# Cross-attention and a two-of-eight expert layer on one core: the hand-over between the two reordered, the places of the rows worked out on two engines

## The chip, the cores and the metric

One Trainium2 chip, one of its cores. The metric is the device time of one launch in microseconds (us): lower is better. The engines are TensorE (PE; its weight loads are listed as PEld), VectorE (DVE), ScalarE (ACT), GpSimd (POOL) and SyncE (SP, which here only issues DMAs). Each engine runs its own instructions in order and waits on semaphores for the others.

## What is computed

```python
# x: 16 x 112 x 256 rows, ctx: 16 x 375 x 256, mask: 16 x 375
x = x + attention(layernorm(x), ctx, ctx, mask, Wq, bq, Wk, bk, Wv, bv, Wo, bo)   # 16 heads of 16
flat = layernorm(x).reshape(1792, 256)
probs = softmax(flat @ router_w)                       # 8 experts
topk_w, topk_idx = top_k(probs, 2)
topk_w = topk_w / clip(topk_w.sum(-1), 1e-9)
h = silu(einsum('td,edf->etf', flat, w1))              # w1: 8 x 256 x 512
y = einsum('etf,efd->etd', h, w2)                      # w2: 8 x 512 x 256
x = x + sum over the two chosen experts of y * topk_w
```

All of it is fp32; products are made from a high and a low part of each operand (three products for one).

## The kernel before

The kernel has three stages. In the first (to about 280 us of the profile) 16 batches pass through an attention pipeline; `turn(b)` on each engine is one batch's share of a software pipeline, in which PE makes the maximum pass of batch b+1 (`head_scores`), the scores and outputs of batch b (`quad_scores`, `quad_outputs`, four of each) and the output projection of earlier rows (`project_output`). In the last stage (from about 366 us) 21 expert steps of 256 gathered rows each run on PE, ACT and DVE, with gathers and scatters issued by POOL.

The stage between them is what the change is about. The 1792 rows lie as 14 tiles of 128 rows. They are taken in eight units: six of two tiles, two of one (`UNITS`, line 63). A unit goes through these steps, each in order on its engine:

- PE `project_output(u)` (L1393 is the line of `product`, which issues nearly all matmuls), DVE `residual(u)` (L1091) adds it to `x2`.
- DVE `row_stats` (L1098) and `row_vars` (L1106, L1108) make mean and variance. They are made in four `GROUPS` (line 64): units 0 to 3 together, then 4 and 5, then 6, then 7. POOL `roots(g)` (L652) takes the roots of a group.
- POOL `normalise_rows(u)` (L661) writes units 0 to 5 into one of three buffers `xn2`, DVE `normalise_late(u)` (L1140) units 6 and 7. SP `write_rows` (L510) writes them to DRAM, where the expert steps gather them.
- PE `flat_transpose(u)` (L1546), ACT `flat_high(u)` (L860), DVE `flat_low(u)` (L1146), PE `route(u)` (six matmuls of 8 columns a tile), DVE `read_logits(u)` (L1152).

Then come the choices and the places. DVE `find_two` (L1173 to L1182, the helper `first_of` at L1166 to L1169) finds the two experts of each row, for the early tiles (the first `EARLY_NT` = 12) and for the late ones (2). PE `rank_early` and `rank_late` (L1677, L1680, L1690 to L1694) count rows before each row of the same expert. DVE `place_rows` (L1200 to L1209) turns that into a lane (a block of 128 places) and a place in it. Both are turned into matrices of zeros and ones: `placed`, one instruction for each tile and choice, 28 in all, by POOL `lanes` (L670), and `is_place` by DVE `places_in_block` (L1214). PE `fill_lanes` multiplies them (L1705, 28 matmuls into one bank). Then DVE `read_lanes` (L1238), PE `list_rows` (L1713) and DVE `list_tokens` (L1243, L1244) give the list by which POOL `gather_rows` (L706) fetches rows.

What sets the order is written by hand: each engine's list of calls behind its attention turns (DVE from L1312, PE and ACT likewise). On PE the list of the last turn alternates attention and router calls; on PE its tail is:

```python
            route(6)
            rank_early()
            flat_transpose(7)
            route(7)
            fill_lanes(slice(0, EARLY_NT))
            rank_late()
            fill_lanes(slice(EARLY_NT, NT))
            list_rows()
```

So `rank_late` stands behind the early `fill_lanes` on PE, and that waits for all of POOL's early lanes: POOL signals `lanes_ready` once for each part. SP loads all experts' weights in two DMAs of 4 MB, the first when the last scores are made, the second behind the writes of units 4 and 5.

## Time and profile before

| | us |
|---|---|
| median of 3 runs | 538.22 (536.15 to 539.46) |
| the profiled execution, its own time | 534.11 |
| its span from first to last instruction | 532.4 |
| mean granted TensorE clock | 0.876 of full speed |
| busy in the span: PE, DVE, ACT, POOL | 428.3, 344.4, 261.0, 235.2 |

The span is that of the one profiled execution; 1.7 us of its time lie outside it. Its own time lies below all three timed runs, so a difference read from its rows is taken as a difference, not as a level.

### The profile page before, as it was taken

To read this page: it belongs to the slowest core of one execution; us is meant where nothing else is said; L and a number is where in the kernel's file an instruction comes from. 1 tells how busy PE (TensorE), PEld (TensorE's weight loads), DVE (VectorE), ACT (ScalarE), POOL (GpSimd) and SP (SyncE) were. 2 spreads that over 40 slices of the span, in tenths; PEclk is the share of its full clock that TensorE was granted. 3 is DMA by queue.
4 is the path that set the end of the run, shared out by engine and by line. 5 is a ranking of instruction groups with operands and counts; after the bars stand their busy time and mean duration, and the time that the engine had idled before them with its cause. 6 is when DMAs were issued, how large, how long until landed. Compare 5 with 4: busy or idle time off the path is not lost.

```text
span 532.4 us, 10679 instructions
## 1 busy us (share of the span) xinstructions
PE 428.3 (80%) x4181; PEld 396.3 (74%) x4181; DVE 344.4 (65%) x748; ACT 261.0 (49%) x332; POOL 235.2 (44%) x206
## 2 busy tenths in 40 slices
PE   2657889999999999799998976041798999999920
PEld 2544689999999899699997875041698999999820
DVE  2776567878787788688777135405468677676617
ACT  3331056666666666466555210001676887788700
POOL 7270352222222222024705700955458777887430
PEclk9796679999999999999999655555899999999975
DMA  7859558677676677965500694001212222233148
GB/s 184 205 153 297 179 132 167 137 140 151 142 151 135 127 158 173 223 125 119 118 2 24 236 367 148 0 0 30 70 60 71 91 89 80 86 94 81 50 139 314
DMA packets 58227, 69.83 MB, mean 131 GB/s; under 512 B 18977, under 2 KB 51506, under 8 KB 58178
## 3 DMA queue, kind: packets, MB, share of 16 engines
q1 hardware_dynamic: 52242, 56.30, 43.4%
q0 software_dynamic: 4032, 11.02, 7.0%
q10 hardware_dynamic: 1904, 1.84, 1.0%
q8 instruction: 33, 0.54, 0.4%
q14 instruction: 16, 0.13, 0.1%
HBM read 35.64 MB, written 14.78 MB: 95 GB/s over the span
## 4 chain that ended last, share of the span: by engine, by line
PE 68%; DVE 11%; POOL 7%; issue 7%; DMA 3%; ACT 2%; DVEq 0%; POOLq 0%; ACTq 0%; SPq 0%
PE ps L1393 36%; PE ps L1454 11%; PE ps L1483 8%; PE ps L1469 8%; POOL placed L670 4%; DVE x L1383 2%; PE ps L1722 2%; PE ps L1496 1%; DVE x_rows_sb L1026 1%; PE ps L1546 1%; DVE neg_max L979 1%; POOL xn L661 1%; DVE stats L1015 1%; DMA y_back<-y_rows 1%; DVE stats L1098 1%
## 5 line engine op out<-in xcount | busy, mean ns | idle before, releaser
L979 DVE TENSOR_REDUCE neg_max<-ps 112x1 f32<-112x376 f32 x256 | 133.8, 546 | 41.4 <-PE ps L1454 36.7
L775 ACT ACTIVATE probs<-ps 125x1344 f32<-125x1344 f32 x64 | 82.7, 1292 | 43.3 <-PE ps L1469 38.1
L1454 PE MATMUL ps<-k_stack,q_stack 98*112 98x376 f32 x256 | 88.4, 381 | 12.0 <-issue 8.6
L560 POOL TENSOR_TENSOR k_lo<-k_f,k_hi 128x752 fp32r<-128x752 f32 x16 | 28.8, 1803 | 132.0 <-ACT k_hi L749 129.6
L1454 PEld LDWEIGHTS ps<-k_stack,q_stack 98*112 98x112 f32 x256 | 45.7, 181 | 25.3 <-DVE neg_max L979 12.2
L714 POOL DMA_INDIRECT y_rows<-y_out,slot_of_row x42 | 48.3, 1150 | 31.6 <-ACT y_out L924 21.2
L706 POOL DMA_INDIRECT rows<-xn_rows,token_of_row x42 | 52.1, 1239 | 16.9 <-issue 12.2
L1469 PE MATMUL ps<-q_stack,k_stack 100*125 100x224 f32 x384 | 53.1, 274 | 0.4 <-DMA q_stack<-max_rows 0.4
L1469 PEld LDWEIGHTS ps<-q_stack,k_stack 100*125 100x125 f32 x384 | 51.1, 190 | 1.1 <-DMA q_stack<-max_rows 0.6
L1393 PE MATMUL ps<-w_hi,h_hi 128*128 128x256 f32 x168 | 49.1, 292 | 3.2 <-issue 1.6
L1393 PE MATMUL ps<-flat_t_hi,w_hi 128*128 128x256 f32 x168 | 47.6, 284 | 4.4 <-DVE flat_t_lo L1277 4.4
L1483 PE MATMUL ps<-probs,v_wide 125*32 125x112 f32 x1536 | 48.1, 266 | 0.9 <-ACT probs L775 0.9
L1393 PE MATMUL ps<-w_hi,h_lo 128*128 128x256 f32 x168 | 47.6, 283 | 0.0
L1393 PE MATMUL ps<-w_lo,h_hi 128*128 128x256 f32 x168 | 47.5, 283 | 0.0
L1393 PE MATMUL ps<-flat_t_hi,w_lo 128*128 128x256 f32 x168 | 47.2, 281 | 0.0
L1393 PE MATMUL ps<-flat_t_lo,w_hi 128*128 128x256 f32 x168 | 47.1, 280 | 0.0
L1483 PEld LDWEIGHTS ps<-probs,v_wide 125*32 125x32 f32 x1536 | 35.9, 111 | 9.5 <-issue 6.3
L1299 DVE TENSOR_TENSOR h_lo<-h_f,h_hi 128x1024 fp32r<-128x1024 f32 x21 | 25.7, 1225 | 24.1 <-ACT h_hi L910 13.6
L899 ACT CAST w_hi<-w_all 128x1024 fp32r x21 | 22.5, 1069 | 35.2 <-DVE expert_of_step L1260 34.8
L1393 PEld LDWEIGHTS ps<-flat_t_hi,w_hi 128*128 128x128 f32 x168 | 32.3, 192 | 5.3 <-DVE flat_t_lo L1277 5.3
L1393 PEld LDWEIGHTS ps<-w_hi,h_hi 128*128 128x128 f32 x168 | 32.2, 192 | 3.6 <-issue 3.6
L1393 PEld LDWEIGHTS ps<-flat_t_hi,w_lo 128*128 128x128 f32 x168 | 32.3, 192 | 0.0
(191 smaller groups left out, 1047.5 us busy)
## 6 DMA issues: line engine op xcount, KB each, us to landing
k_stack<-k_hi SPq DMA_DIRECT2D x64, 188.0 KB, 4.5
w_all<-w SPq DMA_DIRECT2D x2, 4096.0 KB, 19.3
k_stack<-k_lo SPq DMA_DIRECT2D x32, 188.0 KB, 5.4
ctx_raw<-ctx_t SPq DMA_DIRECT2D x32, 187.5 KB, 5.4
q_stack<-q_scratch SPq DMA_DIRECT2D x32, 168.0 KB
q_scratch<-q_hi SPq DMA_DIRECT2D x16, 224.0 KB, 2.9
y_back<-y_rows SPq DMA_DIRECT2D x7, 512.0 KB, 6.5
q_scratch<-q_lo SPq DMA_DIRECT2D x8, 224.0 KB, 3.0
```

Of the source, the lines that this page charges most:

```text
L560: pool.tensor_tensor(kl[:, :, :], kf[:, :, :], kh[:, :, :].bitcast(F32), ALU.subtract)\
L670: last = pool.tensor_scalar(placed[:, c, n, :], place_no[:, 0:ER], lane_of[:, c, n:n + 1], slot_no[:, c, n:n + 1], ALU.is_equal, ALU.mult)
L706: pool.indirect_dma_start(rows[t.ring][:, a, :], None, xn_rows, row_of(token_i, t, a))\
L714: pool.indirect_dma_start(y_rows, row_of(slot_i, t, a), yo[t.par][:, a, :], None)\
L775: act.activation(pf[j % 2][:, :, :], ps[0:CT, BK_ST:BK_ST + KT, 0:4 * S], ACT.Exp).then_inc(pf_ready, 1)
L899: act.copy(w1h[t.par][:, :, :], w1_all[:, bass.ds(experts[t.n], 1), :] .rearrange("p a (k n) -> p (a k) n", k=KD)).then_inc(w1h_ready, 1)
L979: dve.tensor_reduce(neg_max[:, s:s + 1], ps[0:S, BK_MAX + s % 2, 0:CP], AX.X, ALU.max, negate=True).then_inc(max_read, 1)
L1299: dve.tensor_tensor(hl[t.par][:, :, :], hf[t.par][:, :, :], hh[t.par][:, :, :].bitcast(F32), ALU.subtract).then_inc(hl_ready, 1)
L1393: last = pe.matmul(o, lhs, rhs, start=first and n == 0, stop=final and n == len(terms) - 1)
L1454: pe.matmul(ps[0:S, BK_MAX + a, 0:CP], qs[b.ring][0:R_MAX, q, S * a:S * (a + 1)], ks[b.ring][0:R_MAX, q, :], start=True, stop=True).then_i ...
L1469: last = pe.matmul(ps[0:CT, BK_ST + k3, 2 * S * q:2 * S * (q + 1)], ks[b.ring][0:ROWS, 2 * j + q, k3 * CT:(k3 + 1) * CT], qs[b.ring][0:ROW ...
L1483: last = pe.matmul(ps[VC * i:VC * (i + 1), BK_OUT, S * j:S * (j + 1)], vx[b.par][:, k3, 2 * j + i // 2 + HALF * (i % 2), :], pf[j % 2][:, ...
```

## The change

The stage between attention and experts is rewritten; attention's turns 2 and 14 and the stage's helpers are touched.

- Statistics and roots are made for each of the eight units by itself; those of units 0 and 1 move into DVE's turn 14. The constants that DVE set behind the turns (L1312 to L1322) move to the head of its turn 2.
- Six buffers `xn2` in place of three; the three new ones lie where `is_place` comes later, so `places_in_block` waits for their writes.
- PE's, ACT's and DVE's lists of the last turn are reordered: the attention calls first.
- `route` takes the high and low part of the router weights as 16 columns of one matmul: four matmuls a tile in place of six; `read_logits` becomes a reduction that adds the two halves.
- `find_two` takes 12 instructions in place of 13 (and one more wait); the constant that `place_rows` added is added by one more matmul in each ranking.
- `EARLY_NT` is 8 in place of 12: eight early tiles and six late ones.
- POOL makes 11 of the 16 early lanes and 3 of the 12 late ones, DVE the other 5 and 9. `fill_lanes` takes DVE's first, then POOL's one by one. Both rankings stand in front of both fills on PE.

```diff
-GROUPS = ((0, 4), (4, 2), (6, 1), (7, 1))
+XN_RINGS = 6
-BK_PROJ = (5, 6, 5, 6, 5, 6, 0, 1)
+BK_PROJ = (5, 6, 5, 6, 5, 6, 4, 0)
-EARLY_NT = 12
+EARLY_NT = 8
+POOL_LANES = (11, 3)
...
             def normalise_rows(u):
-                pool.wait_ge(row_rstd_ready, 1 if u < 4 else 2)
-                if u >= RINGS:
-                    pool.wait_ge(ft_done, u - RINGS + 1)
-                    pool.wait_ge(xn_written[u % RINGS], 16)
+                pool.wait_ge(row_rstd_ready, u + 1)
+                if u == RINGS:
+                    pool.wait_ge(st_done, QUADS * (B - 1))
...
+            def lanes(part):
+
+                pool.wait_ge(lanes_known, part + 1)
+                for c, n in lanes_of(part)[:POOL_LANES[part]]:
+                    pool.tensor_scalar(placed[:, c, n, :], place_no[:, 0:ER], lane_of[:, c, n:n + 1],
+                                       slot_no[:, c, n:n + 1], ALU.is_equal, ALU.mult).then_inc(pool_lanes, 1)
...
-            roots(0)
-            for u in range(0, 4):
+            for u in range(5):
+                roots(u)
                 normalise_rows(u)
-            roots(1)
-            for u in range(4, 6):
-                normalise_rows(u)
-            roots(2)
-            roots(3)
-            lanes(slice(0, EARLY_NT), 1)
-            lanes(slice(EARLY_NT, NT), 2)
+            roots(5)
+            roots(6)
+            normalise_rows(5)
+            roots(7)
+            lanes(0)
+            lanes(1)
...
             def turn(b):
                 after, before = b.after(1), b.after(-1)
+                if b.n == 2:
+                    set_constants()
+                if b.n == B - 2:
+                    row_vars(0)
...
                 else:
+                    if b.n == B - 2:
+                        row_vars(1)
                     residual(2 * (b.n - B + 3) + 0)
...
-                step(dve.tensor_tensor(t0[:, tiles, :], src[:, tiles, :], wide2(col, tiles), ALU.is_equal))
-                step(dve.tensor_tensor(t1[:, tiles, :], t0[:, tiles, :], pos[:, tiles, :], ALU.mult))
+                step(dve.scalar_tensor_tensor(out=t1[:, tiles, :], in0=less[:, tiles, :], scalar=0.0,
+                                              in1=pos[:, tiles, :], op0=ALU.is_equal, op1=ALU.mult))
...
-            row_vars(0, row_stats(3))
+            row_vars(2)
+            flat_low(0)
+            row_vars(3)
             normalise(last.after(-1))
             residual(4)
-            row_stats(4)
+            row_vars(4)
             attn_low(last.after(-1))
-            residual(5)
-            row_vars(1, row_stats(5))
-            flat_low(0)
             read_logits(0)
             flat_low(1)
+            residual(5)
+            row_vars(5)
+            residual(6)
+            row_vars(6)
             read_logits(1)
+            normalise(last)
             flat_low(2)
+            normalise_late(6)
+            attn_low(last)
+            flat_low(3)
             read_logits(2)
+            residual(7)
+            row_vars(7)
             read_logits(3)
+            find_two(early_tiles, 4)
+            count_early()
             flat_low(4)
+            flat_low(5)
             read_logits(4)
+            normalise_late(7)
             read_logits(5)
             flat_low(6)
+            flat_low(7)
+            place_rows(0, early_tiles, BK_RANK)
             read_logits(6)
             read_logits(7)
             find_two(late_tiles, 8)
+            lanes(0)
             for c in range(TOP):
                 places_in_block(c, early_tiles)
+            place_rows(1, late_tiles, BK_LATE)
             for c in range(TOP):
                 places_in_block(c, late_tiles)
+            lanes(1)
             count_blocks()
...
+                    for k in range(KD):
+                        pe.matmul(ps[:, BK_FLAT[u % 2], 2 * E * a:2 * E * (a + 1)], fh[u % 2][:, k, m], rw[:, k, :],
+                                  start=k == 0, stop=False)
+                        last = pe.matmul(ps[:, BK_FLAT[u % 2], 2 * E * a:2 * E * a + E], fl[u % 2][:, k, m],
+                                         rw[:, k, 0:E], start=False, stop=k == KD - 1)
...
+                pe.wait_ge(places_ready, TOP * (part + 1))
+                pe.wait_ge(dve_lanes, dve_before + len(on_dve))
+                for a, (c, n) in enumerate(on_dve):
+                    last = fill(c, n, part == 0 and a == 0, False)
+                for a, (c, n) in enumerate(on_pool):
+                    pe.wait_ge(pool_lanes, (0 if part == 0 else POOL_LANES[0]) + a + 1)
+                    last = fill(c, n, False, part == 1 and a == len(on_pool) - 1)
...
```

PE's new list in full, from its last turn on (`before` is batch 14, `last` batch 15):

```python
            quad_outputs(before, 2); flat_transpose(0); quad_outputs(before, 3)
            quad_scores(last, 0); out_transpose(before); project_output(4); attn_transpose(before)
            quad_scores(last, 1); quad_outputs(last, 0); route(0)
            quad_scores(last, 2); flat_transpose(1); quad_outputs(last, 1); project_output(5)
            quad_scores(last, 3); quad_outputs(last, 2); project_output(6); quad_outputs(last, 3); route(1)
            out_transpose(last); flat_transpose(2); flat_transpose(3); attn_transpose(last); route(2)
            project_output(7); route(3); flat_transpose(4); flat_transpose(5)
            rank_early(); route(4); route(5); flat_transpose(6); flat_transpose(7); route(6); route(7)
            rank_late(); fill_lanes(0); fill_lanes(1); list_rows()
```

## Rows read from the trace of the kernel before

**Rows 1.** The page: busy share in 40 slices of 13.3 us, and the granted clock.
```profile
PE   2657889999999999799998976041798999999920
...
PEclk9796679999999999999999655555899999999975
```

**Rows 2.** Busy time of each engine in stretches of 10 us.
```profile
core 0: us, PE busy (x) PEld busy (x) DVE busy (x) ACT busy (x) POOL busy (x), PEclk, DMA share, GB/s
295.00:305.00 10.00, 9.28 (x78) 7.84 (x78) 1.64 (x4) 2.36 (x5) 8.24 (x7) 0.50 0.72 241
...
335.00:345.00 10.00, 0.00 (x0) 0.00 (x0) 4.18 (x7) 0.00 (x0) 10.00 (x11) 0.50 0.00 0
345.00:355.00 10.00, 1.42 (x8) 1.42 (x8) 0.00 (x0) 0.00 (x0) 8.52 (x12) 0.50 0.00 0
```

**Rows 3.** The chain that ended last, by time: start, us, what.
```profile
276.12 1.44 PE ps L1393 x12
...
313.86 2.39 PE ps L1393 x12
...
333.08 20.45 POOL placed L670 x24
353.52 6.87 issue
...
360.45 3.17 POOL placed L670 x4
...
363.66 1.02 PE ps L1705 x4
...
391.29 5.62 PE ps L1393 x48
```

**Rows 4.** Who waited for whom, 332 to 372 us: us, times, longest.
```profile
PE ps L1705 <- POOL placed L670: 25.3, 2, 20.7
...
DVE gate L1200 <- PE ps L1694: 19.8, 1, 19.8
```

**Rows 5.** POOL's lanes, by tile: duration min/median/max in ns.
```profile
L670 POOL TENSOR_SCALAR placed<-numbers,lane_of x28: 731/731/3866, 333.1 to 362.9; 128x112 fp32r<-128x112 f32 x28
```

**Rows 6.** VectorE by time: statistics, normalising, choices, places.
```profile
291.43 0.75 DVE L1098 BATCH_NORM_STATS2 stats<-x 128x6 f32<-128x256 f32 x2
292.22 0.38 DVE L1106 BATCH_NORM_AGGREGATE moments<-stats 128x2 f32<-128x6 f32 x4
...
316.96 0.40 DVE L1140 TENSOR_SCALAR xn<-x,moments,row_rstd 128x256 f32<-128x256 f32 x1
...
325.14 0.26 DVE L1178 SCALAR_TENSOR_TENSOR gate<-chosen_experts,gate 128x96 f32<-128x96 f32 x1
...
335.18 0.18 DVE L1167 TENSOR_TENSOR gate<-gate,gate_pos 128x16 f32<-128x16 f32 x1
...
335.90 3.42 DVE L1214 TENSOR_TENSOR is_place<-in_block,numbers 128x1536 fp32r<-128x1536 f32 x2
```

**Rows 7.** TensorE by time, at both clocks: attention, ranking, filling, first expert step.
```profile
280.20 1.36 PE L1483 MATMUL ps<-probs,v_wide 125*32 125x112 f32 x48
...
286.14 0.89 PE L1469 MATMUL ps<-q_stack,k_stack 100*125 100x224 f32 x6
...
302.24 1.35 PE L1483 MATMUL ps<-probs,v_wide 125*32 125x112 f32 x24
...
327.50 2.47 PE L1680 MATMUL ps<-both_experts,ones 128*128 128x88 f32 x11
...
353.58 4.74 PE L1705 MATMUL ps<-is_place,placed 128*112 128x128 f32 x24 [20.70 <-POOL placed L670]
...
375.93 0.41 PE L1393 MATMUL ps<-flat_t_hi,w_lo 128*128 128x256 f32 x1
376.15 0.41 PE L1393 MATMUL ps<-flat_t_lo,w_hi 128*128 128x256 f32 x1
```

**Rows 8.** The page: the weights' load, us from issue to landing.
```profile
w_all<-w SPq DMA_DIRECT2D x2, 4096.0 KB, 19.3
```

More of the change, by code:

```diff
@@ L83, in last_batch, with lanes_of @@
     return (P * tiles_of(u).stop - 1) // S
+def lanes_of(part):
+    tiles = (range(EARLY_NT), range(EARLY_NT, NT))[part]
+    return [(c, n) for c in range(TOP) for n in tiles]
 class Batch:
@@ L127, in xattn_moe_kernel @@
         rw_raw = sb("router_raw", [P, KD, E])
[L128 to L129 removed]
+        rw = sb("router_parts", [P, KD, 2 * E], F32R)
+        reach = sb("reach", [1, E], F32R)
         bo_b = sb("bo_b", [P, D])
@@ L246, in xattn_moe_kernel @@
         cursor["at"] = xr_at
+        xn2 += [sb(f"xn2_{p}", [P, 2, D]) for p in range(RINGS, XN_RINGS)]
+        cursor["at"] = xr_at
         is_place = sb("is_place", [P, TOP, NT, P], F32R)
@@ L864, in _ @@
                 turn(Batch(0, b))
-            end, last = Batch(0, B), Batch(0, B - 1)
+            last = Batch(0, B - 1)
+            flat_high(0)
             out_copy(last.after(-1))
             exps(last, 0)
+            attn_high(last.after(-1))
             exps(last, 1)
-            attn_high(last.after(-1))
             exps(last, 2)
-            flat_high(0)
+            flat_high(1)
             exps(last, 3)
-            flat_high(1)
+            out_copy(last)
             flat_high(2)
-            out_copy(last)
-            flat_high(3)
-            flat_high(4)
             attn_high(last)
-            flat_high(5)
-            flat_high(6)
-            flat_high(7)
+            for u in range(3, len(UNITS)):
+                flat_high(u)
             def rows_high(t):
@@ L1099, in row_stats, with row_vars @@
                 return last
-            def row_vars(g, last):
-                first, n = GROUPS[g]
-                tiles = slice(tiles_of(first).start, tiles_of(first + n - 1).stop)
-                step(last)
+            def row_vars(u):
+                tiles = tiles_of(u)
+                step(row_stats(u))
                 for n in range(tiles.start, tiles.stop):
@@ L1345, in _ @@
+            count_early()
             flat_low(4)
-            attn_low(last)
+            flat_low(5)
             read_logits(4)
-            flat_low(5)
-            normalise_late(6)
+            normalise_late(7)
             read_logits(5)
-            residual(7)
-            row_vars(3, row_stats(7))
             flat_low(6)
-            find_two(early_tiles, 6)
-            count_early()
-            normalise_late(7)
+            flat_low(7)
+            place_rows(0, early_tiles, BK_RANK)
@@ L1504, in attn_transpose @@
                     pe.wait_ge(tl_ready, KD * b.n)
+                    if not has(b.after(1)):
+                        pe.wait_ge(resid_added, 7)
                 for k in range(KD):
@@ L1678, in rank_early @@
                           start=True, stop=False)
+                pe.wait_ge(sel_set, 1)
+                pe.matmul(ps[:, BK_RANK, 0:wide].rearrange("p (n e) -> p n e", e=E), ones[0:1, :],
+                          reach.rearrange("p (a e) -> p a e", a=1).to_broadcast([1, EARLY_NT, E]), start=False, stop=False)
                 for n in range(EARLY_NT - 1):
@@ L1691, in rank_late @@
                           .to_broadcast([P, late + 1, E]), start=True, stop=False)
+                pe.matmul(cols[:, 0:late, :], ones[0:1, :],
+                          reach.rearrange("p (a e) -> p a e", a=1).to_broadcast([1, late, E]), start=False, stop=False)
                 pe.matmul(cols[:, 0:late, :], earlier[:, :], both[:, EARLY_NT:NT, :], start=False, stop=False)
@@ L1697, in rank_late, with fill_lanes, fill @@
                 last.then_inc(ranked, 1)
-            def fill_lanes(tiles):
-                pe.wait_ge(lanes_ready, 1 if tiles.start == 0 else 2)
-                for c in range(TOP):
-                    pe.wait_ge(places_ready, (0 if tiles.start == 0 else TOP) + c + 1)
-                    for n in range(tiles.start, tiles.stop):
-                        last = pe.matmul(ps[0:ER, BK_PLACED, 0:P], placed[:, c, n, :], is_place[:, c, n, :],
-                                         start=c == 0 and n == 0, stop=c == TOP - 1 and n == NT - 1)
-                if tiles.stop == NT:
+            def fill_lanes(part):
+                def fill(c, n, first, final):
+                    return pe.matmul(ps[0:ER, BK_PLACED, 0:P], placed[:, c, n, :], is_place[:, c, n, :],
+                                     start=first, stop=final)
+                both_choices = lanes_of(part)
+                on_pool, on_dve = both_choices[:POOL_LANES[part]], both_choices[POOL_LANES[part]:]
+                dve_before = 0 if part == 0 else TOP * EARLY_NT - POOL_LANES[0]
+                pe.wait_ge(places_ready, TOP * (part + 1))
[5 more added lines that the diff above has]
+                    last = fill(c, n, False, part == 1 and a == len(on_pool) - 1)
+                if part == 1:
                     last.then_inc(lanes_filled, 1)
```

174 lines of the change are left out of this document (82 added, 92 removed).

## The prediction

> **What bounds the kernel now.** I read the slices first. PE is busy at 9 tenths through attention and again through the expert steps, and between them lies a hole: digits 6, 0, 4, 1 at a granted clock of 0.5 [rows 1]. The stretches say what stands in the hole: from 335 to 345 us PE does nothing, DVE 4.18 us and POOL all 10 [rows 2]. The chain of waits gives its pieces: 24 POOL lanes for 20.45 us, then 6.87 us in which the early fill (4.74 us), the late ranking and DVE's places pass one after another, then four more lanes for 3.17 us and four fills for 1.02 us [rows 3, 7]. So from 333.1 to 364.7 us, 31.6 us, the hand-over hangs on POOL's lanes. The waits agree: PE's fill waits 25.3 us for lanes, and DVE waits 19.8 us for a late ranking that needs no early lane and only stands behind the early fill on PE [rows 4]. Behind 364.7 us come the list, the gather and 21 expert steps that the change leaves alone. What decides is therefore when the last fill ends: at 364.7 us before. I walk the new order to that point.
>
> **A: the rest of attention, to about 297 us.** I start at 279.8 us, where turn 14 ends on PE in the old trace. From 282.4 us PE has four scores at 0.82 each (0.89 for six matmuls less their overlap), five outputs at 0.71 (half of 1.36), two output projections of two tiles at 1.44, one of one tile at 0.72, two routings of 8 matmuls at 0.9, two unit transposes, an out and an attention transpose of together 2.2 us [rows 3, 7]. That is 3.3 + 3.6 + 2.9 + 0.7 + 1.8 + 2.2 = 14.5 us. The one long wait in it is for the row maxima's DMA, about 0.1 us less than 1; ACT's four exponentials fit beside it. So PE ends route(1) at about 297. Before, this attention work was spread to 308 us, partly at half clock: 24 output matmuls took 0.71 us before and 1.35 us behind 295 us [rows 7], a stretch with clock 0.50 [rows 2]. The clock fell there among router matmuls of 8 columns and waits for POOL. In the new order these stretches hold attention's matmuls, so I take the full clock up to 297 us and half of it from there.
>
> **B: to the fourth logits, 304.7 us.** The chain is out_transpose and normalise(15) 1.4, transposes of units 2 and 3 and attn_transpose 1.9, the two ACT and DVE parts of attention's last rows with flat_low(2) and normalise_late(6) between them 1.9, project_output(7) 1.3 at half clock, and route(3): 8 matmuls at 0.2 (12 took 2.39) 1.7 with its handing on [rows 3]. Sum: 8.2 less 0.5 of overlap, so 304.7. The statistics of each unit (0.75 + 0.2 + 0.15 and handing on, 1.25 us) and the late ones (0.85) [rows 6] lie beside PE's attention work; if that cover went, three of them, some 3 us, would show.
>
> **C: to both logits of the last tiles, 317.3 us.** find_two for 8 tiles is 12 steps on 64 elements. A step costs 0.29 from start to start at 96 elements and 0.21 at 16 (durations 0.26 and 0.18 [rows 6]), so 0.256 here: 3.1 us, to 307.8. rank_early is 9 matmuls at 0.21 (11 took 2.47): to 309.8. Then route(4) and (5), 3.5 us, to 313.3; the two single transposes with ACT and DVE 1.6, routes 6 and 7 at 0.85 each, to 316.6; DVE's place_rows(0) (five steps, 1.4 us) stands in front of the two reads, to 317.3. The added reductions in read_logits cost under 0.1 us each; bounds 0 and 0.1.
>
> **D: the tail, DVE in front.** find_two for 6 tiles: 12 steps at 0.24 = 2.9, to 320.1. rank_late (9 matmuls, 2.0) hides behind DVE's next work. Five lanes on DVE: the trace has no such instruction. The nearest is the same operation on 256 elements, 0.40 us, and the shortest with 16 elements is 0.18 [rows 6]; at 112 elements I take 0.27 and 0.20 from start to start, bounds 0.18 and 0.40. That gives 1.0, to 321.1. is_place for 8 tiles is two thirds of 3.42 = 2.3, to 323.4; place_rows(1) 1.4, to 324.8; is_place for 6 tiles 1.7, to 326.6; nine lanes 1.8, to 328.4. POOL: 11 lanes from 316.8. A lane alone takes 0.731 us, and the one beside the two is_place took 3.87 [rows 5], so POOL stood still for nearly all of their 3.42 us [rows 6]. I price 11 x 0.73 + 2.3 + 1.7 = 12.0, to 328.9, and three more 2.2, to 331.1. PE's fills are 0.2 each (24 in 4.74 [rows 7]); nine follow DVE's last lane, to 330.2, and the last of POOL's ends at about 331.3. POOL and DVE end within a microsecond of each other.
>
> **E: what is pushed.** Statistics of unit 0 stand in front of the maxima of turn 14, 1.25 us with 0.44 us idle there to take them (before 267.3 in the same timeline); PE has hardly an idle moment in that turn, so +0.8. The constants in turn 2 are 0.7 us of memsets (281.5 to 282.2 in DVE's timeline): between 0 and 0.7, I take 0.4. Statistics of unit 1 fit into a wait for the projection: 0 to 0.5, I take 0. The constants and unit statistics that left the place at 281.5 us are in the walk. For some 60 handings on that I have rounded I add 1.0. The last fill then ends at 331.3 + 0.8 + 0.4 + 1.0 = 333.5 us against 364.7: 31.2 us less.
>
> Against the profile's own time that is 534.1 - 31.2 = 502.9. All three timed runs lie above that execution, so for the median I take the difference from theirs: 538.2 - 31.2 = 507.0.
>
> **What stays hidden.** The weights' DMAs now start at about 294 and 300 us; before they took 19.3 us to land [rows 8] and started at 298 and 304. The first expert cast comes at about 338, 12 us behind their landing; without that cover each microsecond would show. DVE's new wait for three row writes stands in front of its first is_place, with rows queued since 300 us at the latest, and 20 us of room; behind it stand everything on DVE and the late lanes of POOL.
>
> **Rivals.**
> - *The port works both ways.* Rows show that POOL waits for DVE's is_place. In the old trace the late find_two, with two-input steps, ran beside lanes at 0.21 us a step [rows 6], so DVE didn't wait in turn. If it does here, some 8 steps of find_two and four is_place each wait for a lane of 0.73: 12 x 0.73 = +8.8, 515.8. The Trainium skill ("SBUF — State Buffer", Who interferes with whom) states that a DVE instruction with two SBUF inputs and a GpSimd one that reads SBUF exclude each other, and that whoever comes first holds the ports for its whole instruction. On POOL's side the trace agrees (3.87 us); on DVE's side it does not.
> - *The clock falls earlier.* For it: the old clock fell at 295 us after PE waits of only about 1 us, and the new order has one near 283 us. Against it: attention's turns have kept the full clock through such waits. Then A runs at half clock, ratio 1.9, partly under ACT: +10 us, 517.
> - *A hidden transfer comes late* (row writes or weights) *or the statistics lose their cover:* +5 to +10 us, 514.
> - *It ends slower than before.* The clock comes back late in the expert steps. At half clock a matmul there takes 0.21 us, at full 0.117 (48 in 5.62) [rows 3, 7], and there are 21 x 48. The loss is 0.095 x 48 = 4.6 us a step, so from the seventh step at half clock on the gain is gone; with all 21, 603 us. Before, it rose within the first step, at 377 us, and the steps are dense from their beginning.
> - *It does not do what it says:* DVE lanes cost as much as POOL's, and the tail is no shorter. 14 x 0.73 in place of 2.8 gives +7.4, 514.4, so even this leaves most of the gain.
>
> **How the numbers follow.** Forecast, with its bounds (the rounding, the DVE lanes up to +2.8, E up to 1.5 more, 3 less if the clock holds through C): 0.82. Port both ways 0.05, clock early 0.05, cover or transfer late 0.04, dear DVE lanes 0.02, slower 0.02. The median of so few runs moves by one or two microseconds. The range 502 to 515 leaves out the far ends of the rivals and some of either tail. A difference of 1% (5.4 us) is what a measurement of this kernel can tell. Faster by over 1%: 0.97; within: 0.01; slower: 0.02.
>
> **What would show it.** Right: the last fill at 331 to 336 us; PE's wait for lanes under 8 us in all; the late ranking within 3 us of DVE's find_two; POOL lanes of 0.73 with a few long ones beside is_place; 166 to 168 us from last fill to end, as before. Wrong: half clock ahead of 295; DVE lanes over 0.4 us; DVE's places waiting for row writes; a first expert step that waits for weights; or a hand-over that ends past 342 us.

## The result, and the profile after

| | before | changed |
|---|---|---|
| median, us | 538.84 (536.15 to 542.29, 4 runs) | 504.70 (501.91 to 505.92, 4 runs) |
| the profiled execution, its own time, us | 534.11 | 503.95 |
| its span, us | 532.4 | 501.8 |
| mean granted clock | 0.876 | 0.903 |

The ratio of the medians is 0.9356, with a 95% interval of 0.9288 to 0.9424. The changed kernel was measured once more beside the experiments, against eleven runs of the kernel before: 504.67 us, ratio 0.9383 (0.9335 to 0.9431). So the change takes some 34 us; 507.0 was forecast.

The slices of the changed kernel, 12.5 us each:

```profile
PE   2676689999999999979999998546899999999810
...
PEclk9795769999999999998999996557999999999975
```

The hole between attention and the expert steps is still there, but it has become short: 5, 4, 6 where [rows 1] had 6, 0, 4, 1, and the granted clock is at 0.5 for two slices. The stretches of the stage show where the level changes (columns: stretch, length, busy us and instructions of PE, PEld, DVE, ACT and POOL, granted clock, DMA share, GB/s):

```profile
295.00:300.00 5.00, 5.00 (x79) 4.41 (x77) 3.74 (x11) 2.21 (x3) 1.49 (x2) 1.00 0.33 78
300.00:305.00 5.00, 4.38 (x37) 3.94 (x37) 3.55 (x10) 1.66 (x4) 2.97 (x3) 1.00 1.02 385
305.00:310.00 5.00, 3.21 (x15) 2.72 (x14) 4.42 (x20) 1.17 (x2) 0.57 (x1) 0.51 1.04 380
310.00:315.00 5.00, 5.00 (x25) 4.99 (x24) 1.42 (x4) 0.00 (x0) 0.00 (x0) 0.50 1.09 374
...
325.00:330.00 5.00, 3.44 (x16) 3.06 (x16) 4.79 (x15) 0.00 (x0) 5.00 (x5) 0.50 0.01 2
```

Against [rows 2] the reader sees two things. Attention's last rows run at the full 2.4 GHz up to 305 us, where the clock before had gone to 1.2 GHz at 295. And the stretch from 325 to 330 has DVE at 4.79 us and POOL at 5.00 side by side, where from 345 to 355 us before POOL had been busy and DVE not at all. The chain that ended last, in the tail of the stage (start, us, what):

```profile
318.17 0.18 DVE in_block L1229
...
321.92 1.11 DVE placed L1235 x4
323.03 2.35 DVE is_place L1243 x2
...
326.71 1.85 DVE is_place L1243 x2
328.56 2.33 DVE placed L1235 x9
330.88 0.14 issue
331.02 2.48 PE ps L1730 x12
333.53 0.30 DVE lane_tokens L1267
```

DVE carries the chain through the tail, until PE makes the last twelve fills behind DVE's last lane. The 20.45 us of POOL lanes, the 6.87 us of ranking and handing on, and the 3.17 us of late lanes of [rows 3] are gone from it, and the last fill ends 333.5 us into the span instead of 364.7. The waits from 282 to 335 us that answer to [rows 4] (us in all, times, the longest):

```profile
PE ps L1716 <- DVE both_experts L1204: 3.4, 1, 3.4
...
PE ps L1730 <- DVE is_place L1243: 1.3, 1, 1.3
...
PE ps L1730 <- POOL placed L677: 1.1, 2, 0.7
...
PE ps L1730 <- DVE placed L1235: 0.7, 1, 0.7
```

PE's fills (L1730) wait 3.1 us in all, of which 1.8 for lanes, where they had waited 25.3. The late ranking (L1716) now waits only for DVE's own `find_two`. The instructions of the tile `placed` on both engines (minimum, median and maximum in ns, first and last start):

```profile
L677 POOL TENSOR_SCALAR placed<-numbers,lane_of x14: 737/782/2299, 318.2 to 331.4; 128x112 fp32r<-128x112 f32 x14
L1235 DVE TENSOR_SCALAR placed<-numbers,lane_of x14: 325/358/397, 321.7 to 330.5; 128x112 fp32r<-128x112 f32 x14
```

POOL's price is that of [rows 5]. DVE's, which no row of before showed, is 0.36 us; its groups of nine and of five lanes take 2.40 and 1.36 us, so 0.26 from start to start.

### The profile page after: what moved, and what is told of

It reads as the page before. It is cut to its first block, busy times and chain, and to the rows that moved or that the text cites. A ratio compares the mean times of both kernels' runs of the same rounds, so it can differ in the third digit from the quotient of the medians.

```text
span 501.8 us, 10633 instructions
## 1 busy us (share of the span) xinstructions
PE 422.1 (84%) x4155; PEld 389.5 (78%) x4155; DVE 349.4 (70%) x762; ACT 260.4 (52%) x332; POOL 226.1 (45%) x197
## 4 chain that ended last, share of the span: by engine, by line
PE 71%; DVE 14%; issue 6%; DMA 4%; ACT 2%; POOL 2%; DVEq 0%; POOLq 0%; SPq 0%; ACTq 0%
PE ps L1412 36%; PE ps L1473 11%; PE ps L1488 9%; PE ps L1502 8%; DVE x L1402 2%; PE ps L1758 2%; PE ps L1515 1%; DVE x_rows_sb L1028 1%; DVE neg_max L981 1%; DVE is_place L1243 1%; DVE stats L1017 1%; DMA y_back<-y_rows 1%; PE ps L1577 1%; DVE placed L1235 1%; DMA q_stack<-max_rows 1%
## 5 line engine op out<-in xcount | busy, mean ns | idle before, releaser
L1473 PE MATMUL ps<-k_stack,q_stack 98*112 98x376 f32 x256 | 89.6, 384 | 13.0 <-issue 8.6
L711 POOL DMA_INDIRECT rows<-xn_rows,token_of_row x42 | 53.9, 1284 | 17.3 <-issue 12.2
L719 POOL DMA_INDIRECT y_rows<-y_out,slot_of_row x42 | 45.3, 1078 | 33.5 <-ACT y_out L926 22.1
L1412 PEld LDWEIGHTS ps<-flat_t_lo,w_hi 128*128 128x128 f32 x168 | 32.6, 194 | 0.0
```

Source lines behind the costliest of these rows:

```text
L711: pool.indirect_dma_start(rows[t.ring][:, a, :], None, xn_rows, row_of(token_i, t, a))\
L719: pool.indirect_dma_start(y_rows, row_of(slot_i, t, a), yo[t.par][:, a, :], None)\
L1412: last = pe.matmul(o, lhs, rhs, start=first and n == 0, stop=final and n == len(terms) - 1)
L1473: pe.matmul(ps[0:S, BK_MAX + a, 0:CP], qs[b.ring][0:R_MAX, q, S * a:S * (a + 1)], ks[b.ring][0:R_MAX, q, :], start=True, stop=True).then_i ...
```

## The experiments

Each run is judged by three numbers of its profile. The *start* is where DVE begins to read the row maxima of the last batch; the *stage* runs from there to DVE's read of the filled lanes; the *rest* is what is left of the span. The medians alone mislead, since the rest, in which the code is the same everywhere but for e8 and e9, took 166.4 to 178.0 us (last section). And e1, e3, e4 and e6 ran on another chip than c0 and the others, with the kernel before at 541.46 us beside them, against 538.71 beside the others. The three numbers are those of one profiled execution for each row. In us:

| run | start | stage | rest | span | median |
|---|---|---|---|---|---|
| before | 280.1 | 84.6 | 167.7 | 532.4 | 538.8 |
| changed | 283.5 | 50.1 | 168.3 | 501.8 | 504.7 |
| c0 changed, second measure | 283.6 | 48.9 | 168.7 | 501.2 | 504.7 |
| e1 lanes all on POOL | 281.3 | 58.8 | 178.0 | 518.1 | 519.8 |
| e2 lanes all on DVE | 286.6 | 52.9 | 168.1 | 507.6 | 509.5 (one) |
| e3 six router products | 282.5 | 54.3 | 172.2 | 509.0 | 512.9 |
| e4 grouped statistics | 283.2 | 58.4 | 175.8 | 517.4 | 519.4 |
| e5 before, ranking first | 282.9 | 80.4 | 168.7 | 532.0 | 533.7 (one) |
| e6 e5 and shared lanes | 284.5 | 69.0 | 168.7 | 522.3 | 524.8 |
| e7 `x2` in pieces | 278.8 | 50.2 | 168.2 | 497.2 | 499.4 |
| e8 filler matmuls | 283.6 | 47.7 | 166.4 | 497.7 | 501.0 |
| e9 e7 and e8 | 279.6 | 47.7 | 166.6 | 493.9 | 495.2 |
| e10 constants late | 284.2 | 50.1 | 168.5 | 502.8 | 504.6 (one) |
| e11 twelve early | 284.1 | 51.5 | 168.9 | 504.5 | 506.7 (one) |

**The changed kernel once more.** No edit.

> The changed kernel as it is, as the measure for the three beside it on the same chip. The stage from the row maxima of the last batch to the reading of the lanes took 50.1 us in its first profile; a second should say 50 +- 1 if that stage is a fixed cost, and the whole 0.930 to 0.942 of the kernel before.

Measured: 504.67 us (502.52 to 507.99, six runs), ratio 0.9383, as expected; stage 48.9, just outside 50 +- 1.

The two measures of the changed kernel scatter by 1.2 us in the stage. The whole gain there is 84.6 less 50.1 or 48.9, 34.5 to 35.7 us. My theory shares it out: the tail (lanes on two engines, late ranking first) gives about half, and the order and clock of attention's last turn with the router's fewer instructions the rest. A difference of the stage that is not clearly over 1.2 us is not told from scatter here. The rivals of the prediction, a port that works both ways and a clock that falls early, are asked for in e1, e2, e3 and e4.

**The tail alone, on the kernel before (e6).**

```diff
 EARLY_NT = 12
+POOL_LANES = (12, 1)
...
-            fill_lanes(slice(0, EARLY_NT))
             rank_late()
-            fill_lanes(slice(EARLY_NT, NT))
+            fill_lanes(0)
+            fill_lanes(1)
```

(`lanes` and `fill_lanes` are those of the changed kernel; DVE's lanes stand in front of its `is_place`, and behind the late ones.)

> The kernel before with two edits of the tail alone: rank_late in front of both fills, and the lanes shared (POOL 12 of 24 early and 1 of 4 late, DVE 12 and 3). Twelve early tiles, old statistics, old order, old router. Theory: the last fill ends at about 347.9 us in place of 364.7: 17 us less than before, 522 us; so the tail's edits carry half of the gain, and the reordering with the early statistics, the clock and the eight early tiles the other half. Rival (the lanes were nearly all of it): 27 us less or more, 511 us.

Measured: 524.81 us, ratio 0.9725 (0.965 to 0.9801) to 541.46 us of seven runs of the kernel before beside it: −16.7 us. The stage is 69.0, which is 15.6 less than before, where 16.8 was expected. The tail alone gives under half of the gain; it can't explain the whole.

**The order of the ranking alone, on the kernel before (e5).**

```diff
-            fill_lanes(slice(0, EARLY_NT))
             rank_late()
+            fill_lanes(slice(0, EARLY_NT))
             fill_lanes(slice(EARLY_NT, NT))
```

> The kernel before with one edit: rank_late in front of both fills on PE. Theory: POOL's four late lanes follow the 24 early ones without the pause of 6.9 us in which the early fill stood in front of the late ranking; PE then fills 24 (4.7 us) behind the last early lane and four more, so the last fill ends 4 to 5 us earlier: the stage takes 80 us where it took 84.6. Rival (the whole of the 6.9 us goes): 77.7 us.

Measured: stage 80.4, −4.2 us (a single time, 533.73). Its chain of waits shows what is left:

```profile
337.04 15.02 POOL placed L670 x17
352.06 0.64 issue
352.71 5.06 POOL placed L670 x7
357.77 0.04 issue
357.81 5.50 PE ps L1705 x28
363.34 0.30 DVE lane_tokens L1238
```

PE now stands behind POOL's signal, given once for each part, and then makes all 28 fills in a row. The wait of 19.8 us that the profile showed on the late ranking [rows 4] was therefore mostly cover for lanes that would have been late anyway. Of e6's 15.6 us this order brings 4.2, sharing the lanes and signalling each of them 11.4.

**All lanes on POOL, in the changed kernel (e1).**

```diff
-POOL_LANES = (11, 3)
+POOL_LANES = (16, 12)
...
```

(`fill_lanes` is adapted to a share of DVE's that is empty.)

> The new kernel with all 28 lanes on POOL (POOL_LANES = (16, 12)), all else as changed. Theory (the hand-over ends where the lanes end, and sharing them is worth its arithmetic): POOL runs 28 lanes of 0.78 us from 318.2 us and stands still beside DVE's four is_place (4.2 us), so its last lane ends at about 344.3 and the last fill at 344.8 us against 333.5: +11 us, 516 us. Rival (the split is worth little, the gain came from the reordered calls and eight early tiles, which give POOL an early start): +0 to +3 us, 505 to 508 us.

Measured: stage 58.8, +8.8 to +9.9 against the two measures, a little less than expected. The median, 519.81, ratio 0.9627 (0.9555 to 0.9699), is 15.1 us above that of the changed kernel, more than expected; its profile has the rest 9.3 to 9.7 longer and the start 2.2 to 2.3 earlier. POOL's lanes:

```profile
L677 POOL TENSOR_SCALAR placed<-numbers,lane_of x28: 729/736/2563, 316.0 to 338.8; 128x112 fp32r<-128x112 f32 x28
```

The price of a lane is the same, and DVE's read waits for the last of them. Against POOL alone, sharing them is worth some 9 us here.

**All lanes on DVE (e2).**

```diff
-POOL_LANES = (11, 3)
+POOL_LANES = (0, 0)
...
```

(`lanes` and `fill_lanes` are adapted to a share of POOL's that is empty.)

> The changed kernel with all 28 lanes on DVE (POOL_LANES = (0, 0)). The measured price of a DVE lane is 0.26 us from start to start. Theory: 14 more of them stand in DVE's chain and nothing of POOL's comes off it, so the stage from the last row maxima to the reading of the lanes takes 3.2 to 3.8 us more than 50.1: 53.5. Rival (POOL's ports cost DVE more than its lanes save): the two-input steps get faster without POOL beside them, and the stage takes 49 to 51 us.

Measured: stage 52.9, +2.8 to +4.0 (one time, 509.45), so beside DVE, POOL's help is worth 3 to 4 us. With e1 this says that of the 9 us some 6 come already from taking all lanes off POOL (58.8 to 52.9). This run also answers the port rival, since POOL is idle beside DVE here. DVE's lanes, then one two-input step of the late `find_two` in this run, and the same step of the changed kernel with POOL at a lane beside it:

```profile
L1236 DVE TENSOR_SCALAR placed<-numbers,lane_of x28: 331/332/335, 324.4 to 336.5; 128x112 fp32r<-128x112 f32 x28
```

```profile
322.15 0.21 DVE L1188 SCALAR_TENSOR_TENSOR gate<-gate,gate_pos 128x48 f32<-128x48 f32 x1
```

```profile
319.15 0.33 DVE L1187 SCALAR_TENSOR_TENSOR gate<-gate,gate_pos 128x48 f32<-128x48 f32 x1
```

Alone the step takes 0.21 us, beside POOL 0.33 this time and 0.24 at its second place; of the eight two-input steps four kept their 0.21 us beside POOL and four took 0.24 to 0.33. Over all 12 steps the late `find_two` took 2.85 us without POOL and 3.1 with it. The rival asked for 0.73 us at each of 12 instructions, some eight of `find_two` and the four `is_place`, 8.8 in all. What there is of it is 0.25 us in `find_two`, and under 0.1 in `is_place` (2.43 and 1.85 us for the pairs, 2.35 and 1.83 without POOL). A lane on DVE is 0.33 us alone and 0.36 beside POOL.

**Six router products as before (e3).** The high and low parts of the router weights are no longer side by side in one matmul of 16 columns, and the logits are copied in place of added up:

```diff
-                dve.tensor_reduce(logits[:, tiles_of(u), :], ps[:, BK_FLAT[u % 2], 0:2 * E * UNITS[u][1]]
...
+                dve.tensor_copy(logits[:, tiles_of(u), :],
...
-                    for k in range(KD):
-                        pe.matmul(ps[:, BK_FLAT[u % 2], 2 * E * a:2 * E * (a + 1)], fh[u % 2][:, k, m], rw[:, k, :],
-                                  start=k == 0, stop=False)
-                        last = pe.matmul(ps[:, BK_FLAT[u % 2], 2 * E * a:2 * E * a + E], fl[u % 2][:, k, m],
-                                         rw[:, k, 0:E], start=False, stop=k == KD - 1)
+                    last = product(ps[:, BK_FLAT[u % 2], E * a:E * (a + 1)],
+                                   [(x[u % 2][:, k, m], rw[:, k, c]) for k in range(KD)
+                                    for x, c in ((fh, slice(0, E)), (fh, slice(E, 2 * E)), (fl, slice(0, E)))])
```

> The new kernel with six router matmuls of 8 columns a tile and the logits copied, as before. Theory: each two-tile unit takes four matmuls more; routes 4 and 5 (0.85 us each at half clock) and routes 6 and 7 (0.43 each) lie on the path, the earlier ones mostly beside DVE and POOL: +2.5 to +3.5 us, 507.5 us. Rival (router matmuls of few columns are what makes the clock fall): the clock falls ahead of 305 us, as far forward as the first router call at 292 us, and attention's rest runs at half clock: +8 us or more.

Measured: stage 54.3, +4.2 to +5.4, more than expected. The clock was the question here, and it held to about the place of the changed kernel's first measure (the stretch answers to the second one shown for it):

```profile
300.00:305.00 5.00, 4.38 (x37) 4.00 (x35) 3.51 (x10) 1.67 (x4) 1.95 (x2) 0.97 1.03 387
```

In the new order, router matmuls of 8 columns do not bring the fall earlier. Of what they cost, the 12 more of routings 4 to 7, at 0.21 us each, are 2.5 us on the chain; the shares of the others, at full clock, and of scatter were not parted.

**Grouped statistics as before (e4).** Units 0 to 3 get their statistics together when all are there, and one root for all:

```diff
-                if b.n == B - 2:
-                    row_vars(0)
...
-                    if b.n == B - 2:
-                        row_vars(1)
...
-            row_vars(2)
+            first_vars()
             flat_low(0)
-            row_vars(3)
```

(POOL's `roots` are changed to match; PE's list stays that of the changed kernel.)

> The new kernel with the statistics and roots of units 0 to 3 made together behind attention's last full turn, as before, the new order of calls kept. Theory (the new order stands only on early statistics): the first normalised rows come at about 292.6 us, PE's first transpose stands at 284.8 in front of attention's calls, so PE waits some 7.5 us; with the clock falling in that wait another 1 to 5 us: +7 to +12 us, 512 to 517 us. Rival (statistics are off the path, the gain comes from the tail alone): +0 to +1 us.

Measured: stage 58.4, +8.3 to +9.5; median 519.35, ratio 0.9621 (0.9543 to 0.9699). The wait and the stretches around it:

```profile
PE ps L1574 <- POOL xn L670: 8.0, 1, 8.0
```

```profile
285.00:290.00 5.00, 0.00 (x0) 0.00 (x0) 3.00 (x16) 0.46 (x1) 1.68 (x1) 0.94 0.01 2
290.00:295.00 5.00, 2.38 (x29) 1.72 (x29) 0.61 (x1) 0.58 (x1) 4.89 (x5) 0.50 0.15 52
295.00:300.00 5.00, 5.00 (x58) 4.71 (x56) 2.32 (x8) 3.20 (x5) 4.78 (x4) 0.88 0.31 105
```

PE stands 8.0 us for POOL's first normalised rows, and the clock is then at 0.50 until dense attention work has brought it back to 0.88. Here the clock fell behind a stand of 8 us, with the router matmuls of 16 columns; in e3, with those of 8 columns and no such stand, it didn't. So here it was the stand, and not the width, that went ahead of it.

The price is one of the new order. There PE's first transpose stands in front of attention's calls, so late statistics stop all that is behind it. In the kernel before, with the same grouping, PE's longest wait from 281 to 300 us was this:

```profile
PE ps L1546 <- POOL xn L661: 1.0, 1, 1.0
```

So e4 says what the new order needs, and not what the grouping had cost the kernel before. That is also why no wait of 8 us can be what lowered the clock at 295 us there. e5 and e6 have the code of before up to this place, with the same longest wait of 1.0 us, and fell later, e5 from 295 to 300 and e6 from 300 to 305 us:

```profile
295.00:300.00 5.00, 4.20 (x50) 3.81 (x50) 2.33 (x9) 2.35 (x3) 5.00 (x5) 0.92 0.32 108
```

```profile
300.00:305.00 5.00, 4.56 (x41) 4.04 (x42) 1.19 (x3) 0.77 (x2) 4.90 (x5) 0.59 0.59 142
```

Counted from the start of the stage, the fall came after about 15 us in the profile before and 16 in e5 and e6, and in the new order after 22 (first measure, e3), 24 (e1) and 28 (second measure). That the rewritten last turn puts it later is shown; what in the old order brings it earlier stays open.

**The parting at twelve early tiles (e11).**

```diff
-EARLY_NT = 8
-POOL_LANES = (11, 3)
+EARLY_NT = 12
+POOL_LANES = (13, 1)
...
-            find_two(early_tiles, 4)
-            count_early()
             flat_low(4)
...
             read_logits(5)
+            find_two(early_tiles, 6)
+            count_early()
```

(PE's `rank_early` moves behind `flat_transpose(7)`.)

> The changed kernel with twelve early tiles and two late ones, lanes (13, 1) on POOL, find_two of the early tiles behind the sixth logits and rank_early behind the last transpose. Theory (the split of eight and six is small beside the order and the lanes): the walk gives the last fill within 1.5 us of where it is; the stage takes 50 to 52 us. Rival (eight early tiles are what starts POOL early enough): POOL's lanes then start and end later, 55 us or more.

Measured: stage 51.5, +1.4 to +2.6 (one time, 506.68). A small part, of the size of the scatter.

**The constants, in their place of before (e10).**

```diff
-                if b.n == 2:
-                    set_constants()
...
             last = Batch(0, B - 1)
+            set_constants()
             row_vars(2)
```

> The changed kernel with DVE's constants back behind the attention turns. In turn 2 they cost 0.75 us, nearly their own length, in the profile of the changed kernel. Theory: turn 2 gets 0.75 us shorter, and behind the turns they delay the statistics of units 2 and 3 by 0.7 us, which PE does not wait for: the stage grows by 0 to 0.3, so 0.5 us less in sum. Rival (they cost the same there, since DVE stands in the chain ahead of normalise): no difference in sum.

Measured: turn 2 of the first stage takes 13.70 us against 14.47 in the changed kernel and 13.73 before, so the memsets do push PE by 0.75 us there. The stage went from 48.9 or 50.1 to 50.1, between nothing and +1.2, which is no more than the scatter of the changed kernel itself. The price in turn 2 is shown, the balance isn't.

**`x2` in pieces (e7).** The changed kernel's start came 3.3 us later than that of the profile before, more than the 1.2 of the forecast. Turn by turn, 1.5 us of this lies in one turn, in which `x2` (1792 KB) is loaded in one DMA and PE stands 3.1 us, then goes on at half clock. Seven pieces, from turn 3 on, so that both the size of a load and its time are changed:

```diff
-                if b == 10:
+                if b == 3:
                     sp.wait_ge(qproj_done, 2 * NG)
-                    sp.dma_start(x2[:, :, :], x_tiles.rearrange("n p d -> p n d")).then_inc(x2_in, 16)
+                if 3 <= b < 10:
+                    g = slice(2 * (b - 3), 2 * (b - 3) + 2)
+                    sp.dma_start(x2[:, g, :], x_tiles[g, :, :].rearrange("n p d -> p n d")).then_inc(x2_in, 16)
...
-                    pool.wait_ge(x2_in, 16)
+                    pool.wait_ge(x2_in, 16 * NT // 2)
```

> The changed kernel with the load of x2 (1.8 MB in one DMA at batch 10) cut into seven pieces, one each at batches 3 to 9. Theory: 3.3 us of shift ahead of the hand-over where 1.2 were forecast; 1.5 of it is a stretch at half clock behind PE's wait of 3.1 us for operands queued behind that load. In pieces of 256 KB no wait of PE is long: the wait of 3.1 us and the stretch at half clock go, -3 to -4.6 us against the changed kernel. Rival (the DMA engines are full there anyway and each piece makes its own stall): 0 +- 1 us.

Measured: 499.38 us (498.24 to 499.54, six runs), 5.3 less than the changed kernel beside it (504.67); ratio to before 0.9276 (0.9235 to 0.9318). PE's wait in the changed kernel's first measure (2.8 us in the second), then the stretch from 220 to 235 us in its second measure, in this run, and in the profile before:

```profile
PE ps L1473 <- issue: 3.1, 1, 3.1
```

```profile
220.00:235.00 15.00, 12.19 (x152) 10.77 (x154) 8.64 (x19) 7.08 (x11) 3.55 (x2) 0.89 1.04 207
```

```profile
220.00:235.00 15.00, 14.97 (x184) 13.61 (x182) 12.36 (x27) 8.61 (x11) 3.56 (x2) 1.00 0.69 132
```

```profile
220.00:235.00 15.00, 11.96 (x162) 10.79 (x161) 9.24 (x21) 8.29 (x11) 3.59 (x2) 1.00 1.02 196
```

In pieces PE no longer stands and the clock stays full; the turn takes 13.7 us. Whether the smaller size or the earlier time did it isn't shown. It was a stall that both kernels had: 16.8 us for this turn in the profile before, 18.3 in the changed one, 19.3 and 20.6 in e5 and e6, which have the code of before ahead of the stage. Their starts are 282.9 and 284.5. What sets the profile of before apart is the clock: PE stood 3.0 us there too, but the clock stayed full behind it, as it did in only one more of the twelve profiles with the whole load (e1, 16.7 us). So the profile of before, with its start at 280.1, was a lucky execution; its own time, 534.11, is at the lower end of the eleven timed runs of the kernel before beside c0 (534.18 to 541.36).

**Matmuls for nothing but the clock (e8).** A helper makes matmuls of 512 columns into a bank that nobody reads then:

```diff
+            def keep_clock(n):
+                for _ in range(n):
+                    pe.matmul(ps[:, BK_AT, :], ones[:, :], th[:, 0, 0:512], start=True, stop=True)
...
             flat_transpose(5)
+            keep_clock(6)
...
             route(7)
+            keep_clock(12)
             rank_late()
+            keep_clock(4)
             fill_lanes(0)
             fill_lanes(1)
             list_rows()
+            keep_clock(16)
```

> The changed kernel with 38 idle matmuls (128x512, results unread) on PE where it waits between the last output projection and the first gathered rows: 6 ahead of rank_early, 12 and 4 around rank_late, 16 behind list_rows. Theory (half clock from 305 us on costs what hangs on PE in the hand-over, and the first expert step): rank_early, routes 4 to 7 and two transposes cost half, about -4; the last twelve fills -1; the first expert step's 24 matmuls -1.7: -5 to -7 us. Rival (the fillers stand in front of what they should speed up, or the clock falls all the same): 0 to +4 us.

Measured: 501.03 us, −3.6; the stage −1.2 to −2.4, the rest −1.9 to −2.3. Less than expected, and the stretches say why:

```profile
310.00:315.00 5.00, 4.74 (x33) 4.04 (x33) 2.94 (x9) 0.74 (x2) 0.00 (x0) 0.80 1.09 374
315.00:320.00 5.00, 5.00 (x15) 4.14 (x16) 4.41 (x22) 0.30 (x1) 4.01 (x6) 0.52 1.09 349
320.00:325.00 5.00, 4.46 (x30) 3.52 (x28) 4.79 (x13) 0.00 (x0) 5.00 (x5) 1.00 0.87 281
325.00:330.00 5.00, 2.11 (x9) 1.77 (x9) 4.76 (x17) 0.00 (x0) 4.89 (x5) 0.66 0.01 4
330.00:335.00 5.00, 4.62 (x15) 3.77 (x15) 2.77 (x12) 0.00 (x0) 1.27 (x2) 0.50 0.00 0
```

The clock comes and goes. Behind the first six matmuls the routing began at the full clock (0.11 us a matmul at 311 us, against 0.21 in the changed kernel), it fell before that routing's end, and the twelve then ran at half clock, 4.83 us. After them it was full for one stretch, and half again at 330. The matmuls won 1.2 to 2.4 us of the stage; what a clock at full throughout would give isn't measured, and DVE carries the tail.

**Both together (e9),** the diffs of e7 and e8.

> The changed kernel with the load of x2 in pieces and the 38 idle matmuls, the version that I expect to beat both kernels. If the two gains lie in different places they add up: -8 to -11 us against the changed kernel. If they don't add up, one of them is a change of when the clock falls, and the sum is no more than the larger of the two.

Measured: 495.16 us (493.03 to 498.3, six runs), ratio to before 0.9202 (0.9154 to 0.9251), 9.5 less than the changed kernel beside it. The two gains add up (5.3 + 3.6 = 8.9). This version beats both kernels.

**What follows of the sum.** The parts were undone one at a time in the changed kernel: shared lanes 8.8 to 9.9, own statistics 8.3 to 9.5, router columns 4.2 to 5.4, tiles early and late 1.4 to 2.6. That is 22.7 to 27.4. The ranking's order, measured on the old kernel, adds 4.2: 26.9 to 31.6 of 34.5 to 35.7. The sum is no proof that these are the parts. Each was undone with the others kept, and the statistics' 8 to 9 us are a price that only the new order of calls asks. Sharing the lanes brought 11.4 on the old kernel and 8.8 to 9.9 here. Attention first in the last turn, the six buffers and the shorter `find_two` were not measured alone.

## Why the prediction was right

The last fill was forecast at 333.5 us and ended at 333.5. That is closer than the working deserves, since three terms were off and cancel: +1.1 in what is pushed with its rounding, −1.9 in B, +0.9 in D.

- **A, the rest of attention: 17.2 us forecast, 17.2 measured** (283.1 to 300.3). The durations of [rows 3, 7] hold, and so does the full clock. Half clock was assumed from the end of A; it came at 305, 4.8 us behind it.
- **B, to the fourth logits: 7.7 forecast, 5.8 measured.** The step that failed is the clock: I let it fall at the end of A because it had fallen in the old order a little before. With the full clock the output projection took 0.97 where I had taken 1.3, and most of the routing's matmuls 0.11 each where I had taken 0.2. That is not the whole of −1.9. I had put the transposes, 1.9 us, behind out_transpose and normalise(15) on one path; in the trace they ran on PE beside DVE's normalising, and the chain goes by unit 2's transpose and casts:

```profile
300.83 0.45 PE ps L1567 x4
...
301.31 0.59 ACT flat_t_hi L865
...
301.93 0.70 DVE flat_t_lo L1168
...
303.73 0.97 PE ps L1412 x6
...
304.72 0.44 DVE x L1093
```

  This cover hung on the clock as well: eight such matmuls took 1.0 us here and 2.0 at half clock, at 305.6 us. Behind the projection the chain goes by DVE's residual and statistics of unit 7 and not by `route(3)`, whose last matmul ended 0.3 us before they did.
- **C, to the last logits: 12.6 forecast, 12.5 measured.** `find_two` went from step to step in 0.26 (0.256), `rank_early` ran at half clock in 2.3 us, and the routings' matmuls cost 0.21 each.
- **D, the tail: 14.0 forecast, 14.9 measured.** The term that was mis-sized is the DVE lane: 0.20 from start to start taken, inside bounds of 0.18 and 0.40, and about 0.26 measured, 14 x 0.06 = +0.8. With it the path is another than forecast. My sum ended with POOL's lanes, which took 13.9 us where 14.3 were forecast, and it let nine fills follow DVE's last lane, 1.8 us. In the trace DVE's last lane ended 12.3 us behind the last logits (11.1 forecast), and PE made twelve fills behind it, 2.5 us, since POOL's last three stand behind DVE's nine; with the handing on that is 14.9. The rest stands: `is_place` 2.4 and 1.9 (2.3 and 1.7), POOL's lanes 0.74 each and a few long ones beside `is_place`, up to 2.3. POOL's last lane ended 1.3 us behind DVE's and was ready before its fill came.
- **E, what is pushed: +1.2 forecast, and 1.0 of rounding.** The start came 3.3 us later. The constants take 0.75 (0.4 forecast, e10), the statistics of unit 0 0.6 (0.8 forecast: turn 14 takes 15.3 us against 14.7, and 14.7 again in e4), together 1.35, so the term itself was right to 0.2. The other 2.0 is not the change's, as far as the profiles tell: 1.5 lies in the turn of the `x2` load, where the profile before is one of two that kept the full clock. I had read it as typical there.
- **The rest:** 168.3 us measured, 167.7 taken over from before. The weights stayed hidden.
- **The median:** by their own times the two profiled executions are 30.2 us apart, by the medians 34.1. The difference goes with the lucky start of the old profile; the stage's 34.5 to 35.7, less the 1.35 pushed, is 33.2 to 34.3, and agrees with the medians. The forecast took 31.2 off the median of before, 2 to 3 too little: its stage gained 33.4 (84.6 less 51.2), 1.1 to 2.3 under the measured gain, through B above all, and it took back 2.2 for what is pushed and for rounding, where 1.35 was real.

The rivals: the port both ways is refuted as to size (e2: some 0.3 us of 8.8). The clock fell later than forecast, not earlier; e3 shows that router matmuls of 8 columns don't pull it forward in the new order, and why it fell at 295 us in the old one stays open (e4, e5, e6). No transfer of the hand-over came late. The clock came back in the expert steps as before (0.7 in the slice behind the hole, then 0.9). A DVE lane cost 0.06 us more than forecast, where the rival of dear lanes asked for 0.53; e1 shows what POOL's price on all lanes would have been, some 9 us.

## What to carry to other kernels

Where one engine stamps out many small tiles that another consumes one by one, give half of them to the engine that stands idle beside it and signal each; here this was worth 9 us against the slower engine alone and 3 to 4 against the faster alone. When the consumer's calls are moved forward, move what feeds them too: in the new order, statistics made in one group cost 8 to 9 us, since PE stood 8.0 us in front of them. When a wait is removed, walk the whole way to the next hand-over: moving the ranking alone took 4.2 us out of a wait listed with 19.8. And compare more than one execution before a difference ahead of the changed place is put down to the change: a stall that differs from one execution to the next moved it by 2 to 4 us.

## What the runs showed of the hardware

- **Two engines beside each other at short instructions.** POOL's lane goes from 0.74 to 2.3 us beside `is_place`; of DVE's eight two-input steps of 0.21 us in the late `find_two`, four took 0.24 to 0.33 beside lanes and four stayed at 0.21, none 0.74 longer. So POOL pays and DVE pays hardly at all. The Trainium skill ("SBUF — State Buffer", Who interferes with whom) states that a DVE instruction with two SBUF inputs contends with a GpSimd one that reads SBUF, that the ports they share are an exclusive lock, and that the issue order decides who blocks. POOL's side agrees (2.3 us, above). DVE's does not: its short steps began while POOL was at a lane, and lost 0.25 us over 12 steps. The measurement decides.
- **The clock's fall has scatter.** In two executions of the same kernel it fell at 305 and at about 311 us. The second measure of the changed kernel, to be set beside the third stretch of the result:

```profile
305.00:310.00 5.00, 2.27 (x17) 1.81 (x17) 4.39 (x20) 1.17 (x2) 0.56 (x1) 1.00 1.04 391
```

  From 300 to 305 us PE had been busy 4.38 us in both. The stage differed by 1.2 us; that the fall is the reason isn't shown.
- **One load of 1792 KB** had PE stand 2.6 to 4.4 us in the twelve profiles that have it. Behind the stand the clock went to 0.50 in ten of them, and stayed full in two, before and e1, where PE had stood 3.0 us. The turn took 17.8 to 20.6 us in the ten and 16.8 and 16.7 in the two. With seven loads of 256 KB, issued earlier, PE did not stand, and the turn took 13.7 (e7, e9).
- **What stays open.** Behind the reading of the lanes the same code took 167.7 to 168.9 us in most runs, but 172.2 (e3), 175.8 (e4) and 178.0 (e1), all three from the chip of e6, which took 168.7. In e1 three expert steps took 8.4, 9.6 and 11.2 us in place of 6.1, and ACT stood before the transposed rows:

```profile
457.53 0.58 ACT L890 CAST flat_t_hi<-ps 128x512 fp32r<-128x512 f32 x1 [6.35 <-remote]
```

  ACT's cast had to wait for them; why they came late, no run here tells. Because of this all runs, and these three above all, are judged by their stage. Their rests are longer than the changed kernel's by 3.5 to 9.7 us, and by their medians each part would look dearer by 3 to 6 us.
